# Attention and LoRA block on one core: the row sums' inverses stored to DRAM one element at a time, and read back as plain rows

## The reference

```
x = hidden_states                                  # (1, 1024, 512)
h = layernorm(x)
q  = rope(h @ w_q)     32 heads of 128
k  = rope(h @ w_k), v = h @ w_v                    # 8 heads, each used by 4 query heads
lk = rope((h @ w_lq) @ w_lk), lv = h @ w_lv        # 32 "latent" heads
attn = causal_softmax(q k^T / sqrt(128)) v
lat  = causal_softmax(q lk^T / sqrt(128)) lv
x = x + attn @ w_o + lat @ w_lo
x = x + ffn(layernorm(x))                          # one 512x512 product and a routed LoRA
```

## Time and profile before

| | before |
|---|---|
| median of 3 runs | 2168.39 us (2166.27 to 2170.56) |
| profiled execution: its time | 2170.34 us |
| profiled execution: first to last instruction | 2168.5 us |
| mean granted TensorE clock | 0.995 |
| TensorE busy | 2085.7 us, 96% |
| VectorE busy | 1582.2 us, 73% |
| ScalarE busy | 1140.5 us, 53% |
| GpSimd busy | 883.6 us, 41% |
| DMA queue of SP, share of 16 engines | 15.9% |

### The profile page before, as it was taken

How to read it: one execution, slowest core, us unless ns; L and a number is a source line. 1 busy time by engine, 2 the same in 40 slices (tenths; PEclk the granted TensorE clock), 3 DMA queues, 4 the chain that set the end, 5 groups by cost and what they waited for, 6 DMA issues and landing times.

```text
span 2168.5 us, 37857 instructions
## 1 busy us (share of the span) xinstructions
PE 2085.7 (96%) x11236; PEld 1761.5 (81%) x11236; DVE 1582.2 (73%) x2946; ACT 1140.5 (53%) x2502; POOL 883.6 (41%) x693
## 2 busy tenths in 40 slices
PE   5999999999999999999999999999999999999989
PEld 4888878888788887888788887888878888888877
DVE  6677767777777777777777776777777777777775
ACT  2555545555455554555455554555545555555541
POOL 4334443334534344433533444333453334444311
PEclk9999999999999999999999999999999999999999
DMA  2111111111111111112111111111111111111121
GB/s 95 31 35 41 36 32 41 39 39 44 29 41 27 41 46 31 37 36 41 36 36 34 39 37 32 41 41 37 45 27 41 27 41 46 30 41 31 41 50 39
DMA packets 101898, 84.34 MB, mean 39 GB/s; under 512 B 28200, under 2 KB 73896, under 8 KB 101680
## 3 DMA queue, kind: packets, MB, share of 16 engines
q1 hardware_dynamic: 101680, 81.65, 15.9%
HBM read 79.26 MB, written 2.36 MB: 38 GB/s over the span
## 4 chain that ended last, share of the span: by engine, by line
PE 72%; DVE 14%; issue 8%; POOL 3%; ACT 2%; DVEq 0%; DMA 0%; ACTq 0%; SPq 0%; POOLq 0%
PE scores L415 9%; PE scores L417 8%; PE scores L416 8%; PE bankT L477 8%; PE bankX L415 7%; PE bankX L417 7%; PE bankX L416 7%; PE bankO L415 5%; PE bankO L417 5%; PE bankO L416 5%; DVE rot_half L980 3%; DVE rot_half L979 3%; DVE probs L963 3%; DVE PT_lo L969 2%; POOL KT_lo L1191 1%
## 5 line engine op out<-in xcount | busy, mean ns | idle before, releaser
L703 ACT ACTIVATE PT_hi<-bankT 128x512 fp32r<-128x512 f32 (+2 forms) x640 | 336.2, 532 | 413.7 <-PE bankO L417 353.2
L969 DVE TENSOR_TENSOR PT_lo<-bankT,PT_hi 128x512 fp32r<-128x512 f32 (+2 forms) x640 | 387.4, 609 | 184.5 <-ACT PT_hi L703 179.4
L762 ACT ACTIVATE probs<-probs,nmax 128x128 f32<-128x128 f32 (+7 forms) x512 | 394.8, 773 | 140.1 <-DVE nmax L963 139.7
L963 DVE CUSTOM_DVE_ANT_0 probs<-scores,mask 128x128 f32<-128x128 f32 (+7 forms) x512 | 381.1, 750 | 62.2 <-PE scores L417 59.9
L477 PE MATMUL bankT<-ident,probs 128*128 128x128 f32 x2304 | 379.2, 273 | 5.7 <-DVE PT_lo L969 2.2
L477 PEld LDWEIGHTS bankT<-ident,probs 128*128 128x128 f32 x2304 | 285.3, 140 | 73.1 <-DVE PT_lo L969 18.1
L1197 POOL TENSOR_TENSOR rot<-rot,cos 128x512 f32<-128x512 f32 x144 | 185.3, 1287 | 227.8 <-DVE rot_half L980 227.8
L1191 POOL TENSOR_TENSOR OT_lo<-o_raw,OT_hi 128x512 fp32r<-128x512 f32 x64 | 82.7, 1291 | 403.3 <-ACT OT_hi L703 403.3
L1199 POOL TENSOR_TENSOR rot<-rot,rot_half 128x512 f32<-128x512 f32 x144 | 207.3, 1439 | 11.3
L703 ACT ACTIVATE OT_hi<-o_raw 128x512 fp32r<-128x512 f32 x128 | 80.9, 632 | 187.0 <-DVE o_raw L1034 180.5
L979 DVE TENSOR_TENSOR rot_half<-rot,sin 64x512 f32<-64x512 f32 x144 | 108.7, 755 | 82.9 <-ACT rot L703 79.5
(11 more groups left out here) (241 smaller groups left out, 5213.2 us busy)
## 6 DMA issues: line engine op xcount, KB each, us to landing
inv_b<-inverses SPq DMA_DIRECT2D x128, 256.0 KB, 4.1
stage<-in_L_attn_w_q SPq DMA_DIRECT2D x32, 256.0 KB, 4.7
stage<-in_L_attn_w_lv SPq DMA_DIRECT2D x32, 256.0 KB, 2.8
stage<-in_L_attn_w_o SPq DMA_DIRECT2D x32, 256.0 KB, 4.6
stage<-in_L_attn_w_lo SPq DMA_DIRECT2D x32, 256.0 KB, 2.6
acc<-in_L_attn_hidden_states SPq DMA_DIRECT2D x2, 1024.0 KB, 6.6
stage<-in_L_attn_w_k SPq DMA_DIRECT2D x8, 256.0 KB, 4.8
stage<-in_L_attn_w_v SPq DMA_DIRECT2D x8, 256.0 KB, 4.9
```

The costliest lines, as they stand in the source:

```text
L703: return act.activation(place, src, ACT.Copy)
L762: act.activation(prob_tile(c, t), prob_tile(c, t), ACT.Exp, bias=nmax[:, c, t:t + 1], scale=-1.0, accum_out=rsum[:, c, t:t + 1]).then_inc( ...
L963: dve.tensor_tensor_reduce(place, src, tile_view(mask[:, S - width:S], c), -SCALE, -MASKED, ALU.add, ALU.min, nmax[:, c, t:t + 1]).then_in ...
L969: dve.tensor_tensor(pt_place(1, hh, w, j), bankT[j % 2][:, block_columns(c, j):CH], f32(pt_place(0, hh, w, j)), ALU.subtract).then_inc(pt_ ...
```

## The change

The store of the inverses now writes tile by tile: the DRAM row holds the 128 queries of tile 0, then those of tile 1, and so on. A partition's four values no longer lie side by side in DRAM, so the store moves 512 single elements of 4 bytes (its access pattern is 128x4x1 in place of 128x4). The read back is as before, 2 KB for each of 128 partitions. `scale_out` reads `inv_b` as a plain row, and the three operands need no rearranging. No instruction is added, removed or moved on any engine; the number of DMAs stays the same.

```
@@ spread_inverses
-                sp.dma_start(inverses[w % 2].rearrange("(p t) -> p t", p=P), rinv[:, c, :]).then_inc(inverses_stored, 16)
+                sp.dma_start(inverses[w % 2].rearrange("(t p) -> p t", p=P), rinv[:, c, :],
+                             allow_slow_non_contiguous=True).then_inc(inverses_stored, 16)
@@ scale_out
-                dve.tensor_tensor(o_raw[:, w % 2, :].rearrange("p (t q) -> p t q", q=P),
-                                  bankO[:, :].rearrange("p (t q) -> p t q", q=P),
-                                  inv_b[:, w % 2, :].rearrange("p (q t) -> p t q", q=P), ALU.mult).then_inc(o_scaled, 1)
+                dve.tensor_tensor(o_raw[:, w % 2, :], bankO[:, :], inv_b[:, w % 2, :], ALU.mult).then_inc(o_scaled, 1)
```

## The result

| | before | after |
|---|---|---|
| median of the runs, us | 2167.86 | 2341.04 (2339.55 to 2346.61) |
| ratio after / before | | 1.080, interval 1.0785 to 1.0813 |
| span of the profiled execution, us | 2168.5 | 2340.7 |
| granted clock of TensorE, mean | 0.995 | 0.972 |

The kernel became 173 us slower. The forecast was 2148 us, 20 us faster, and its range ended at 2165. What happened is rival C, to which the prediction gave 0.08.

What follows compares the result with a forecast made beforehand. TensorE, busy 96% of the span, was taken as the bound, so VectorE savings count only where it waits. 15.4 + 2.5 + 0.7 = 18.6 us, rounded to 20, store cost 0: 2168.4 - 20 = 2148 us, range 2137 to 2165.

Steps and rivals of the forecast that it cites:

- rival C: Scaling of w0 and w2: store takes over 6.0 us (w2) and 6.8 (w0); at 8 us, 2250 us; chance 0.08.
- Parts 1 and 2: VectorE's scaling falls from 1066 to 692 ns, 48 us of VectorE time; about 20 us of it reaches TensorE.
- w3 to w0: Ordinary heads, TensorE's first PV matmul behind the scaling: 0.14 us lost per head, all recovered.
- w1 to w2: Ordinary heads, third score tile waiting for the first row maximum behind the scaling: 0.30 us per head, all recovered.
- w2 to w3: Transposes behind scaling, OT_lo and PT_lo: 0.20 us per ordinary head; in seven group-last heads 0.34 to 0.37 us.
- A: Waits called covered also shrink, for instance through ScalarE's earlier copies: 2140 to 2120 us, chance 0.12.
- B: The wait goes elsewhere, TensorE meeting the next tile or PT_hi later: 2158 to 2170 us, middle 2165, chance 0.20.
- D: Plain scaling also runs at 1.07 us and nothing moves: 2168 us; its chance is inside B's.
- Part 3: Store of the inverses gets longer, 1.4 to 1.6 us, at most 5.6; covered by the window, so cost 0.
- The rule that spoke against the change: Skill's rule on the store: a strided last dimension becomes one descriptor per element; strided DMA transposes called 19 times slower.
- Cover: Time from store's issue to scaling; less the read's 4.1 us, a store may take 6.0 us in w2, 6.8 in w0.
- seven times a few us: Group-last heads: at a store of 5.6 us, K weights fetched behind the spread could come late, this much in all.

Runs made afterwards that it cites:

- e2: Kernel before with only the plain scaling, old store kept, so inverses meet the wrong queries: 2147.48 us, ratio 0.9901.
- e12: Kernel before plus awaited scratch stores, mostly 128 pieces of 4 bytes at several pitches: 2226.0 us, a time without meaning.
- e6: Changed kernel with its 512 single elements stored 64 bytes apart to a scratch row, inv_b read from a row written once ahead: 2151.58 us, ratio 0.9919.
- e3: Kernel before with only the new single-element store, stepped scaling kept, inverses meet the wrong queries: 2396.37 us, ratio 1.104.
- e7: Changed kernel with the reciprocal that starts the store moved to the end of the window ahead: 2262.66 us, ratio 1.0439.
- e13: Plain scaling; four-column reciprocal, then 32x32 turn, both at the end of the window ahead; store in 128-byte runs: 2150.5 us, ratio 0.9917 to kernel before.
- e8: Plain scaling; VectorE turns the sums in 32x32 blocks, then inverts 32 columns; store in 16 runs of 128 bytes: 2170.19 us, ratio 1.0007 to kernel before.
- e1: Kernel before plus one scratch store per unit behind the read of inv_b, in eight patterns of piece size and spacing: 2168.72 us.
- e5: Kernel before plus awaited scratch stores, among them 512 pieces of 4 bytes at pitches of 4 to 64 bytes: 2301.6 us, a time without meaning.

## Why the prediction was wrong, point by point

**Parts 1 and 2 held.** The scaling takes 681 to 685 ns, and alone it brings 21.0 us where 20 were forecast (e2: 2147.48 against 2168.45). In part that was luck, since the terms were off in both directions: by the mean distance of two scalings in ordinary heads, w3 to w0 gave 0.09 us in place of 0.14, w1 to w2 0.44 in place of 0.30, and w2 to w3 0.03 in place of 0.20, since `OT_lo` stretched beside GpSimd. The group-last heads gave some 0.4 us in w2 to w3, as forecast, and 0.2 in the w0 ahead of it, which wasn't. Rivals A, B and D are out by e2.

**The step that failed is Part 3, the size of the store.** The prediction took +0.2 us from two loads that differ in the number of their pieces, and 5.6 as the upper end, "all of the store's 1.4 us grows fourfold". Both go by count. The rows were of reads, whose pieces were 512 bytes and 2 KB long; no row of the trace had two writes that begin less than 16 bytes apart. A fourfold count is no bound on something that doesn't grow with the count: e12 has 1.4 and 7.7 us for the same 128 writes, 16 and 4 bytes apart. The term was 8.8 in place of 1.6 us.

By the packet records of the changed kernel all 512 pieces of a store have started 1.3 us after the issue (the median; 2.2 at most), and each takes 7 to 9 ns; the semaphore is full 7.5 us later. So the pieces are sent at about the rate that was assumed, and it is their completion that is late. The Trainium skill (DMA: Bandwidth & Descriptors, "Anatomy of one DMA — SWDGE (gpsimd) path") says that the semaphore's update has to wait until the data are written, and that this can take surprisingly long where they go to HBM; the records agree, on another path than the one that page describes there, with 7.5 us.

The rule that spoke against the change, of the Trainium skill (DMA: Bandwidth & Descriptors, "Rules for kernel authors"), was right that the store becomes one descriptor per element (49152 packets more). Its factor wasn't tested. But elements as such are not what cost: e6 stores as many in 2.0 us.

**The second term, which the prediction didn't have,** is the read. It was taken at 4.1 us, and behind the new store it lands in 5.0. The weight loads behind it are later as well.

**The mechanism of rival C was right, and so was its price in a short window; its count of windows was not.** Cover in w0 was 10.9 us from store to scaling, in w2 10.1. Store and read are now 8.8 + 5.0 = 13.8. The lateness by that rule is 2.9 us in w0 and 3.7 in w2; the mean distance from the scaling before grew by 2.9 and 3.5 in ordinary heads. Taken 32 times each, as the prediction does, it is 32 x 6.6 = 211, less the 20, and gives 2359 against 2341 measured. But there are not 32 short windows of each kind. Of the 57 waits of the scaling 48 are those of w0 and w2 in the 24 ordinary heads, with 161 of the 182.6 us. In the group-last heads of the kernel before w2 had 18.6 us from store to scaling, and w1, which the prediction took for long, had 11.4, since its store is issued 4.3 us after the reciprocal; six of the other waits are in that w1.

The distances of the scalings give the whole. In ordinary heads w1 gives back 1.9 us (its window starts late, and part of its work was ready by then; that is argued, not tested) and w3 adds 0.4: 4.9 us a head, 114 us from the first scaling on. In the seven group-last heads with a group behind them w0 costs 6.0 and w1 2.3 us more than before, and w2 and w3 are 1.2 and 0.4 us shorter: 47 us. The last head of all adds 12. Sum: 173.

**The group-last heads** were foreseen as a risk ("seven times a few us") at a store of 5.6. SP's queue and the conversion of the K weights there:

```profile
261.21 0.36 SPq L340 DMA_DIRECT2D inverses<-rinv  x1
270.53 0.33 SPq L344 DMA_DIRECT2D inv_b<-inverses  x1
271.15 0.38 SPq L321 DMA_DIRECT2D stage<-in_L_attn_w_k  x1
```

```profile
276.24 0.63 ACT L704 ACTIVATE Wk_hi<-stage 128x512 fp32r<-128x512 f32 x1 [6.30 <-DMA stage<-in_L_attn_w_k]
```

The K weights are issued behind the read, at 271.15; before, the store was at 248.57 and they followed at 251.64, 3.1 us later, and now it is 9.9 us. ScalarE stands for 6.3 us. Over the eight heads that is the 43.9 us of the waits view.

**The granted clock** wasn't in the sum either. The first PV matmul after the scaling of an ordinary w2 (start, us, what, idle time before and its releaser):

```profile
242.71 0.79 PE L416 MATMUL bankO<-PT_hi,LV_lo 128*128 128x512 f32 x1 [2.67 <-DVE o_raw L1035]
```

TensorE has stood for 2.67 us, and this matmul takes 0.79 us where its like takes 0.5. Not every wait is followed by that: of 35 waits of over 1 us before such a matmul, eight are. In the group-last head the stretches around the late K weights (us, busy us of each engine, granted clock, DMA share, GB/s):

```profile
275.00:280.00 5.00, 0.83 (x5) 0.83 (x5) 1.58 (x3) 2.90 (x6) 1.27 (x1) 0.69 0.26 79
280.00:285.00 5.00, 5.00 (x20) 4.16 (x19) 3.10 (x8) 1.49 (x3) 2.21 (x2) 0.63 0.02 3
285.00:290.00 5.00, 5.00 (x30) 4.30 (x30) 2.57 (x7) 2.59 (x8) 1.56 (x2) 1.00 0.24 53
```

TensorE is busy for 0.83 us of 275 to 280, and the granted clock of that stretch and the next is 0.69 and 0.63, a mixture of the levels 2.4 and 1.2 GHz; at 285 it is full again. In stretches of 5 us from 60 us on, 52 are below 0.97 in the changed kernel and 6 before. The clock taken away in them adds up to 63 and 7 us of full speed, TensorE's idle time within them included. So up to 56 us of the changed kernel's time went with the clock. How much of it reaches the end isn't known, since it lies in windows whose end the store sets anyhow; no run had the waits without the low clock.

**The chances.** 0.08 for C followed from a bound that wasn't one. With the store's price taken as unknown from above, since no row showed a write of this kind, C would have deserved the weight of the forecast, and the cover, 6.0 us, would have been the number to report.

**What stays open:** why writes that begin within 16 bytes of each other are completed so late, and in which unit they queue; why 64 adjacent pieces cost as much as 128 or 512 while 32 cost half; how e3's additional 55 us divide between the ring and the clock; what holds VectorE at the start of a group in e7; and why the read lands sooner behind two stores than behind one.

## What to carry to other kernels

A price of a DMA read off a load or off wider pieces doesn't bound a store of scattered or single elements: the addresses at which the pieces begin have to be compared too, and one probe store beside the kernel tells in a single run what no scaling by count does. Where a transposition must be paid, look for the engine and the window with idle time and pay there (e13), instead of at the place that the saved time was to relieve (e8), and do the arithmetic on the narrow side of the turn. And before pricing a change to a small transfer at nothing, work out its cover and state the length at which it ends; here the lateness by it was right to 0.2 us. The cover has to be taken for each kind of head: the group-last ones differed.

## What the runs showed of the hardware that was not expected

- A store of 4-byte pieces to adjacent DRAM addresses lands 7.3 to 10.2 us after its issue from 64 pieces on (medians of the series of e1, e5 and e12). The same pieces 16 bytes apart land in 1.4 us (128) and 2.8 (512).
- Cutting such a store into eight leaves 6.9 us behind the last issue, and SP needs 3.6 to 7.8 us for eight issues.
- The broadcast read of a row lands later the more finely the row was written just before: 5.0 us after adjacent 4-byte pieces, 4.1 after 16-byte pieces, 3.2 to 3.3 after 128-byte runs or when it wasn't just written.
- VectorE's 128x512 product costs 1066 ns with one SBUF operand at a step of 16 bytes, 1080 ns with the PSUM operand and the result at a step of 512 bytes and that one plain, and 681 to 685 with none.
- Shorter work on VectorE can stretch the next operation: `OT_lo` went from a median of 958 to 1240 ns when it came to lie longer beside GpSimd's addition.
- After TensorE had stood for 2.67 us (w2), and for 4.26 us (the late K weights), its granted clock was below full in the two stretches of 5 us that hold the wait and what follows it: 0.77 and 0.89, and 0.69 and 0.63.
